# One head's scores, row maximum and exponential moved ahead in an attention kernel's hand-written order

## The reference

```python
query = hidden_states @ Wq
keyt, valt = enc @ Wk, enc @ Wv              # enc: 16 x 718 x 384
hs = _mha(query, keyt, valt)                 # softmax(q k^T / sqrt(80)) v, 8 heads
ca_q1 = einsum('btc,th->bch', ca, Wq_ca)[:, indices, :]   # ca: 16 x 4 x 384
ca_hs1 = _mha(ca_q1, residual, residual)
ca_hs2 = _mha(ca_hs1 @ Wq, ca @ Wk_ca, ca @ Wv_ca)
out = (hs + ca_hs2) @ Wout + b_out + residual
```

## Time and profile before

| | us |
|---|---|
| median of 3 runs | 1010.81 |
| lowest, highest | 1004.1, 1011.32 |
| the profiled execution, device time | 1004.1 |
| its span, first to last instruction | 1002.4 |

### The profile page before, as it was taken

How to read it: one execution, slowest core, us unless ns; L and a number is a source line. 1 busy time by engine, 2 the same in 40 slices (tenths; PEclk the granted TensorE clock), 3 DMA queues, 4 the chain that set the end, 5 groups by cost and what they waited for, 6 DMA issues and landing times.

```text
span 1002.4 us, 20729 instructions
## 1 busy us (share of the span) xinstructions
PE 983.8 (98%) x6740; PEld 964.2 (96%) x6740; DVE 645.5 (64%) x1129; ACT 490.0 (49%) x895; POOL 343.5 (34%) x286
## 2 busy tenths in 40 slices
PE   9999799999999999999999999999999999999998
PEld 9998699999999999999999999999999999998997
DVE  6444556676667766767676767676766666667444
ACT  7433445555454546464646463646454545546110
POOL 5212254424251616151524243343343343416000
PEclk9899999999999999999999999999999999999999
DMA  7989967797978797979797978888787878795354
GB/s 266 258 285 279 259 131 203 168 196 172 195 172 191 174 182 178 185 184 179 185 186 176 186 191 169 202 174 201 161 208 157 206 163 202 168 216 156 97 181 146
DMA packets 154169, 190.12 MB, mean 190 GB/s; under 512 B 80928, under 2 KB 108192, under 8 KB 154144
## 3 DMA queue, kind: packets, MB, share of 16 engines
q1 hardware_dynamic: 147456, 177.44, 75.9%
q10 hardware_dynamic: 6688, 12.35, 3.7%
HBM read 81.56 MB, written 19.95 MB: 101 GB/s over the span
## 4 chain that ended last, share of the span: by engine, by line
PE 85%; SPq 5%; DMA 4%; DVE 3%; ACT 2%; issue 1%; ACTq 0%
PE psS L750 22%; PE psB L785 20%; PE psB L790 10%; PE psS L725 8%; PE psT L766 6%; PE psS L894 6%; PE psT L812 4%; PE psT L818 2%; SPq L382 2%; DMA kstack<-kT 1%; PE psB L867 1%; PE psB L844 1%; SPq L379 1%; PE psT L819 1%; PE psS L950 1%
## 5 line engine op out<-in xcount | busy, mean ns | idle before, releaser
L750 PE MATMUL psS<-encT_keep,Wk_keep 128*128 128x360 f32 x1440 | 255.3, 330 | 2.8 <-ACT probs L1133 2.8
L750 PEld LDWEIGHTS psS<-encT_keep,Wk_keep 128*128 128x128 f32 x1440 | 238.7, 189 | 3.9 <-issue 3.3
L785 PE MATMUL psB<-PT_h,encN_h 120*128 120x400 f32 x576 | 202.3, 351 | 0.0
L785 PE MATMUL psB<-PT_l,encN_h 120*128 120x400 f32 x576 | 198.8, 345 | 0.0
L1133 ACT ACTIVATE probs<-psS,negmax 100x718 f32<-100x718 f32 x128 | 110.2, 861 | 131.8 <-DVE negmax L1524 131.6
L612 POOL TENSOR_TENSOR encT_keep<-encT_raw,encT_keep 128x718 fp32r<-128x718 f32 x45 | 79.7, 1770 | 184.6 <-ACT encT_keep L1162 182.2
L1548 DVE TENSOR_TENSOR kT<-psS,kT 128x718 fp32r<-128x718 f32 x80 | 72.4, 905 | 105.7 <-ACT kT L1157 105.7
L620 POOL TENSOR_TENSOR encN_l<-enc_raw,encN_h 120x768 fp32r<-120x768 f32 x48 | 92.4, 1926 | 93.5 <-ACT encN_h L1169 92.1
L603 POOL TENSOR_TENSOR Mbd<-Mbd,fmask 128x320 fp32r<-128x320 f32 x48 | 47.0, 978 | 221.4 <-DMA Mbd<-m_split 218.8
L1157 ACT ACTIVATE kT<-psS 128x718 fp32r<-128x718 f32 x80 | 61.7, 771 | 123.4 <-PE psS L750 109.9
L790 PE MATMUL psB<-PT_h,encN_l 120*128 120x400 f32 x576 | 120.4, 344 | 0.7 <-POOL encN_l L620 0.7
(11 more groups left out here) (245 smaller groups left out, 1635.8 us busy)
## 6 DMA issues: line engine op xcount, KB each, us to landing
kstack<-kT SPq DMA_DIRECT2D x64, 448.8 KB
kstack<-kT SPq DMA_DIRECT2D x192, 112.2 KB
enc_raw<-in_encN_dram SPq DMA_DIRECT2D x48, 360.0 KB, 5.5
encT_raw<-in_encT_dram SPq DMA_DIRECT2D x45, 359.0 KB, 6.0
kstack<-kT SPq DMA_DIRECT2D x32, 359.0 KB
kstack<-kT SPq DMA_DIRECT2D x32, 269.2 KB
kstack<-kT SPq DMA_DIRECT2D x32, 179.5 KB, 3.6
kstack<-kT SPq DMA_DIRECT2D x64, 89.8 KB, 3.9
```

The source lines that it names most:

```text
L750: mm = pe.matmul(keys_in(f, first)[:, half, 0:HALF], w[:, c, f * 128:(f + 1) * 128], e[:, c, k0:k0 + HALF], start=(j == 0), stop=(j == 3 * ...
L785: pe.matmul(psB[:, 1, 0:RH], eN[0][:, k, cc], PT[p][:, k, rows], start=(k == 0 and p == 0), stop=False)
```

## The change

Three edits of order. TensorE runs `scores(i, 5)` directly behind `scores(i, 4)` (in batch 0 behind `query(3, 3)`) and ahead of `b2_turn(i, 1)`, `context(i-1, 5)` and `turn(i, 3)`. VectorE runs `rowmax(i, 5)` two steps earlier, ahead of `b2_pt_low(i, 1)`, and `norm(i, 5)` ahead of `xm_add` and `rowmax(i, 6)`. ScalarE runs `expo(i, 5)` directly behind `b2_pt_high(i, 1)`, and into the old place of `expo(i, 5)` comes `enc_high(i, 1)`, which stood behind `hs_copy(i-1, 1)`. In batch 15 `enc_high(i, 1)` stays where it was. No instruction is added or taken away.

```diff
@@ TensorE batch @@
                     scores(i, 4)
                     if first:
                         query(3, 3)
+                    scores(i, 5)
                     b2_turn(i, 1)
                     if first:
                         query(3, 4)
                     else:
                         context(i - 1, 5)
                     turn(i, 3)
-                    scores(i, 5)
                     b2_xm(i)
@@ ScalarE batch @@
                     b2_pt_high(i, 1)
+                    expo(i, 5)
                     if first:
                         q_high(3, 4)
                         store_q3(3)
@@
                         store_q3(5)
-                    expo(i, 5)
+                    if not last:
+                        enc_high(i, 1)
                     xm_high(i)
                     expo(i, 6)
                     if not first:
                         hs_copy(i - 1, 1)
-                    if not last:
-                        enc_high(i, 1)
@@ VectorE batch @@
                     rowmax(i, 4)
                     if first:
                         q_low(3, 3)
+                    rowmax(i, 5)
                     b2_pt_low(i, 1)
                     norm(i, 4)
@@
                     pt_low(i, 3)
-                    rowmax(i, 5)
+                    norm(i, 5)
                     xm_add(i)
                     if first:
                         q_low(3, 5)
                     rowmax(i, 6)
-                    norm(i, 5)
                     xm_low(i)
```

## The result

| | before | after |
|---|---|---|
| median, us | 1008.17 (16 runs beside after) | 1014.71 (16 runs) |
| lowest, highest | 1004.1, 1012.91 | 1010.76, 1018.54 |
| profiled execution, device time | 1004.1 | 1011.86 |
| its span | 1002.4 | 1010.1 |

The change makes the kernel slower by 0.65%: ratio 1.0065, 95% interval 1.0047 to 1.0083, that is +6.5 us. More runs of the kernel before put its median 2.6 us lower than the three shown ahead of the prediction.

The account below looks back on a forecast made before the run. TensorE, busy 98% of the span, was taken to bound the kernel. Loop +5.9, batch 0 -3.7 and batch 15 -0.5 gave +1.7 us on the median of 1010.81, so 1012 us, range 1001 to 1020.

Parts of the forecast that it names:

- the loop's term: 14 loop rounds: delayed values and late transfer landings cost 0.42 us per round, +5.9 us together, bounds 0 and 9.7.
- `values(i-1, 1)` held by `pt_low(i, 3)`: TensorE in each loop round: values would wait for pt_low and start late, costing 0.29 us per round.
- Rival (a): Loop: it pays nothing, so the kernel takes 1005.6 us; chance 0.21.
- Saved penalty of the scores' new place: TensorE in each loop round: scores(i, 5) avoids a slow first matmul behind short transposes, saving 0.07 us.
- the chain: Loop: enc_high(i, 1) waits for its transfer, GpSimd holds xm_low, then hs_add; turn(i, 4) starts at A + 3.74.
- may also be caught: VectorE in the loop: norm(i, 5) might be held, starting within 0.05 us of enc_low(i, 0); no size given.
- the landings: Loop: transfers for enc_high(i, 1) landing late delay turn(i, 4), lifting the average cost from 0.29 to 0.42 us per round.
- Batch 0: Before the loop: the wait of keys(1, 0) for expo and its slow clock go, gaining 3.7 us, bounds 1.5 and 5.1.
- Rival (b): Batch 0 gives little, as ScalarE or GpSimd replace expo or the clock falls: 1015.7 us, up to 1019; chance 0.20.
- Batch 15: Last batch: hs_add, turn(15, 4) and turn(15, 5) come earlier, -0.5 us, bounds -1.2 and +0.5.
- Rival (c): Loop: later transfers of enc_high(i, 1) make the kernel slower by over 1%, 1022.8 us if 1 us later; chance 0.09.

Follow-up runs that it names:

- Experiment 1: Kernel before with only TensorE's edit, scores(i, 5) directly behind scores(i, 4): 1012.77 us, ratio 1.0034 to the kernel before.
- experiment 7: Changed kernel with turn(i, 3), pt_high(i, 3) and pt_low(i, 3) moved ahead of context(i-1, 5), u_high and u_low: 1009.52 us, ratio 1.0021 to before.
- 3: Changed kernel with enc_high(i, 1) put back behind hs_copy(i-1, 1): 1014.64 us, ratio 1.0064 to the kernel before.
- 4: Changed kernel with norm(i, 5) put back behind rowmax(i, 6): 1014.68 us, ratio 1.0054 to the kernel before.
- experiment 6: Kernel before with the edits in batch 0 only, but enc_high(0, 1) kept in its old place: 1005.14 us, ratio 0.9954.
- experiment 5: Kernel before with all three edits made in batch 0 only, the loop keeping its old order: 1005.13 us, ratio 0.996.
- experiment 8: Changed kernel with enc_high(i, 0) moved behind xm_copy(i) in the loop: 1015.19 us in one execution.
- experiment 2: Kernel before with only enc_high(i, 1) moved ahead of xm_high: 1016.61 us, ratio 1.0078 to the kernel before.

## Why the prediction was right or wrong

Direction and size of the whole: forecast +1.7 us, measured +6.5 (1.0065, within 1%). The median of 1014.71 lies in the range, 2.7 above the 1012 given. That it comes so near is in part luck: the three runs that the prediction started from put before 2.6 us too high, and on that basis of 1010.81 the same ratio would be 1017.4. The change itself was taken 4.8 us too small. The step that failed is the loop's term, forecast +5.9 and measured about +10; the other terms hold or are small.

- **`values(i-1, 1)` held by `pt_low(i, 3)`: right.** Predicted 0.24 + 0.05 = 0.29 us per round, in which the saving of the next point is already taken off. Measured are 0.33 before `values` and 0.06 inside it, less 0.06 saved: 0.33 on the same count. Experiment 1 brings the wait in with TensorE's edit alone, experiment 7 takes it away. Rival (a), that the loop pays nothing, falls with it.
- **Saved penalty of the scores' new place: right.** 0.06 us per round, against 0.07.
- **`turn(i, 4)`: the chain was right for a late landing, and not the one that rules the usual round.** The prediction has `turn(i, 4)` at A + 3.74, A being the start of `enc_high(i, 1)`. In the late round above it is 494.70 + 3.75 = 498.45; in the two others it is 178.38 + 3.76 and 862.93 + 3.75. But in a usual round A is early enough (ScalarE waits 16.6 us at this place in 14 rounds, mean 1.2 us, usually 0.6 to 1.2, where 1.4 was predicted), `xm_low` takes 0.92 us and not 1.6, and another chain arrives last: `norm(i, 5)` held to 2.19 us by `enc_low(i, 0)`, then `rowmax(i, 6)`, `expo(i, 6)`, `hs_copy`, `hs_add`. The prediction took that hold up only as something that "may also be caught" and put no price on it. In the kernel before `hs_add` ended at 442.11 and `turn(i, 4)` could have followed 0.15 later, 1.4 us ahead of its start at 443.70: the hold of 1.6 us uses up this cover. Counted from `turn(i, 3)`, `keys` would let `turn(i, 4)` start at 7.64 in the round shown; `hs_add` ends at 7.61, and the start comes at 7.76. It costs 0.12 in every usual round (3 against 4 show whose it is), and it is what a step-by-step walk through VectorE's queue at 439.9 would have given, from rows that were at hand: `enc_low` starts 0.97 behind its `enc_high`, `norm` follows `pt_low(i, 3)`.
- **The loop's term was mis-sized.** Predicted were 0.42 us per round: 0.29 in every round, and 0.13 on average for the landings. Measured over 13 rounds are 0.67: 0.47 in every round (0.39 at `values`, 0.14 around `turn(i, 4)`, 0.06 saved), 0.10 for late landings and 0.09 for scattered waits. The landings' share was about right; the part that every round pays was too small, by 0.14 that come with the hold of `norm(i, 5)` and by 0.04 at `values` (0.33 against 0.29). Rounds 1 to 14 together cost 10.4 us up to `b2_xm` of batch 15, above the upper bound of 9.7; some 2 of them are scattered waits.
- **Batch 0: right in mechanism, and in size where the profile can say it.** The wait for `expo` and the slow clock are gone. The new wait before L867 is 1.37 us (1.35 predicted). From the last matmul of `query(3, 3)`, just ahead of what was moved, to `b2_scores2(0)` it took 17.01 us before and takes 13.44 now: 3.6 us gained, 3.7 forecast. In experiment 6, where `xm_low` is done before TensorE wants it, it takes 12.15, a gain of 4.9; the bound for that was 5.1. Counted on to the first round's `b2_xm` the gain in after is 3.8. From the start of the span it is only 2.4, since `turn(0, 2)`, ahead of all that was moved, had waited 2.97 us in this execution, 1.27 in that of before, and the stretch behind it, 109.8 to 113.0 us, ran at granted clock 0.55, near the lower level of 1.2 GHz, and not 1.00. That wait was between 0.1 and 3.4 us in the executions profiled, so it is scatter. By times, experiment 5 gives 0.4% or 4.0 us, with an interval from 1.9 to 6.3. Rival (b) is wrong in its cause: batch 0 gave what it promised, and the clock stayed at 1.00 behind the wait of 1.37 us.
- **Batch 15:** -0.5 predicted, about 0 measured. `hs_add` does end earlier, 7.04 instead of 8.76 us behind `b2_xm(15)`, but `turn(15, 4)` starts only 0.14 earlier (8.77 against 8.91): the context step before it waits 0.8 us for GpSimd's `enc_low`, as it did before (0.7). The prediction had not looked at that wait.
- **Rival (c)**, late landings, is what the three late rounds are, but it needed a mean landing 0.6 later than the rows', and the mean stayed where it was, 3.13 us behind `b2_xm` before and 3.10 after.

The SBUF — State Buffer page of the Trainium skill (section "SBUF: two separate sides") lets whichever starts first, a GpSimd instruction or a VectorE one that has two SBUF inputs or runs in a two-port mode, keep the other out for its whole length. The runs agree: 0.04 us behind `enc_low`, `norm(i, 5)` took 2.19 us, and 0.51 us (experiment 8) or 0.17 us (experiment 7) ahead of it 0.59 us. The prediction quoted this rule for two SBUF inputs and weighed it only for `xm_low`. `norm(i, 5)` scales one tensor by a column of numbers, so it may be the other case; which of the two conditions catches it, no run shows. Leaving its hold without a price was the mistake that changed the picture of a usual round. In time it is about 2.0 of the 4.5 us that the loop's term lacked; the scattered waits are another 2.0, `values` 0.6.

## What to carry to other kernels

Before an instruction is moved on VectorE, compare its new start with every GpSimd instruction running at that moment, since 0.04 us decided here over 1.6 us; then walk through what is queued behind it, and subtract the cover. Weigh a wait that is removed once against what every round of the loop pays: here about 4 us were gained once, and 0.47 us or more were lost in each of 14 full rounds. Then make the change only in the part that runs once, as experiments 5 and 6 did (0.996 and 0.9954).

## What the runs showed of the hardware

- A VectorE instruction held by GpSimd's `enc_low` ends 0.28 to 0.29 us after it for `xm_low` (497.83 against 497.55, 440.21 against 439.92), and 0.39 for `norm(i, 5)` in the late round. Its record shows it as busy, not as waiting: VectorE's busy time grew by 32 us with the same 1129 instructions, and the 14 held `norm(i, 5)` alone are 22 of them.
- It goes both ways: when `norm(i, 5)` started 0.17 us ahead, `enc_low` took 2.12 us instead of 1.83.
- After 2.97 us without work TensorE ran the next 3.2 us at granted clock 0.55 (the lower level is 1.2 GHz); after 1.37 us without work the stretch from 128.5 to 131.0 us shows 1.00 (2.4 GHz). The length of one pause does not decide it: in experiment 2 `turn(0, 2)` waited 2.92 us and the stretch from 110.8 to 114.0 us shows 1.00, and in experiment 8 pauses of 0.62 and 0.83 us, at 229.2 and 231.1, were followed by 3.4 us at 0.50. What does decide, these runs don't show.
- The transfers of `enc_high(i, 1)` take 4.4 to 6.0 us from issue to landing in after, 4.1 to 6.3 before, and the engine that waits for them (ScalarE, 0.59 to 2.30 us) passes the late ones on at full size.
